# A four-layer mixer on one core: where VectorE does the three operations of a forget-gate group in the softmax half

## The reference, cut to what matters

```python
x = x + linear_attention(layernorm(x))
x = x + ffn(layernorm(x))
x = x + softmax_attention(layernorm(x))
x = x + ffn(layernorm(x))

def ffn(x):                       # the scan runs over the 8 batches, c is 1024 x 256
    def step(c, xt):
        ft = sigmoid(xt @ wf.T + c @ uf.T + bf)
        it = sigmoid(xt @ wi.T + c @ ui.T + bi)
        gt = tanh(xt @ wc.T + c @ uc.T + bc)
        return ft * c + it * gt, None
    c_final, _ = lax.scan(step, c0, x)
    return tanh(einsum('tbi,oi->tbo', x, wo) + c_final @ uo.T + bo)
```

## Time and profile before

| what | us |
|---|---|
| median of three runs | 2560.55 |
| the profiled execution | 2558.81 |
| its span | 2557.0 |
| TensorE busy (matmul) | 2137.9 (84% of the span) |
| VectorE busy | 1692.4 (66%) |
| ScalarE busy | 1266.0 (50%) |
| GpSimd busy | 781.8 (31%) |
| operations of the gates on VectorE in the softmax half | 96 |

### The profile page before, as it was taken

How to read it: one execution, slowest core, us unless ns; L and a number is a source line. 1 busy time by engine, 2 the same in 40 slices (tenths; PEclk the granted TensorE clock), 3 DMA queues, 4 the chain that set the end, 5 groups by cost and what they waited for, 6 DMA issues and landing times.

```text
span 2557.0 us, 58522 instructions
## 1 busy us (share of the span) xinstructions
PE 2137.9 (84%) x24838; PEld 1215.5 (48%) x24838; DVE 1692.4 (66%) x3766; ACT 1266.0 (50%) x2041; POOL 781.8 (31%) x658
## 2 busy tenths in 40 slices
PE   3558989888897985749889999999999999998954
PEld 1346565655565563424345454454544544444432
DVE  5546475656656455348878788787787877777337
ACT  2414343343424221214666666766676666766723
POOL 2132333414133011143424345243352432412110
PEclk9789999899998988877999999999999999999987
DMA  3201010101011011133324133142331322213053
GB/s 97 66 18 43 26 51 18 58 27 51 18 34 35 18 51 50 43 116 99 115 59 126 52 84 117 47 123 66 85 117 35 117 59 76 76 35 97 38 230 131
DMA packets 131540, 179.28 MB, mean 70 GB/s; under 512 B 9120, under 2 KB 95136, under 8 KB 131280
## 3 DMA queue, kind: packets, MB, share of 16 engines
q1 hardware_dynamic: 129104, 175.02, 22.4%
q10 hardware_dynamic: 2176, 0.52, 0.1%
HBM read 97.40 MB, written 77.59 MB: 68 GB/s over the span
## 4 chain that ended last, share of the span: by engine, by line
PE 63%; DVE 24%; ACT 6%; issue 3%; POOL 2%; DMA 1%; SPq 0%; DVEq 0%; POOLq 0%; ACTq 0%
PE general L893 11%; PE general L579 10%; PE out_of_heads L767 9%; DVE maxima L1428 8%; PE scores L722 6%; PE general L565 4%; PE general L904 4%; PE general L545 3%; PE turned_scores L736 3%; PE out_of_heads L653 3%; PE out_of_heads L663 2%; PE scores L611 2%; PE general L553 2%; DVE probs_turned L1375 1%; PE out_of_heads L787 1%
## 5 line engine op out<-in xcount | busy, mean ns | idle before, releaser
L1428 DVE TENSOR_REDUCE maxima<-scores 128x1 f32<-128x512 f32 (+3 forms) x1536 | 793.9, 553 | 239.4 <-PE scores L698 121.3
L1092 ACT ACTIVATE probs_turned<-turned_scores 128x512 f32<-128x512 f32 x1152 | 680.1, 601 | 373.4 <-PE turned_scores L698 190.7
L722 PE MATMUL scores<-k_stacks,q_stacks 59*128 59x512 bf16 (+3 forms) x1536 | 445.3, 336 | 80.9 <-DVE maxima L1428 74.8
L736 PE MATMUL turned_scores<-q_stacks,k_stacks 61*128 61x512 bf16 (+3 forms) x1536 | 437.5, 330 | 2.2 <-ACT probs_turned L1092 2.2
L722 PEld LDWEIGHTS scores<-k_stacks,q_stacks 59*128 59x128 bf16 x1536 | 123.6, 94 | 313.1 <-DVE maxima L1428 247.9
L1749 POOL TENSOR_TENSOR ln_low<-ln 128x512 bf16<-128x512 f32 x128 | 138.4, 1088 | 279.3 <-DVE ln L1410 255.2
L1728 POOL TENSOR_SCALAR ln<-x_for_attention,ln_mean_var,ln_rstd 128x256 f32<-128x256 f32 x104 | 127.9, 1239 | 186.1 <-DVEq L1516 96.9
L1019 ACT ACTIVATE gate_tanhs<-general,feature_vectors 128x512 f32<-128x512 f32 x96 | 66.0, 687 | 204.2 <-PE general L579 199.9
L1664 POOL TENSOR_TENSOR state_low<-state_doubled,state_high 128x2048 bf16<-128x2048 f32 x14 | 57.0, 4068 | 358.1 <-ACT state_high L1025 358.1
L1393 DVE TENSOR_SCALAR reciprocals<-scores 128x16 f32<-128x16 f32 x64 | 11.1, 173 | 224.5 <-PE scores L671 224.5
L767 PE MATMUL out_of_heads<-probs_turned,values 128*17 128x512 f32 (+3 forms) x1536 | 155.2, 499 | 0.0
(11 more groups left out here) (249 smaller groups left out, 5470.8 us busy)
## 6 DMA issues: line engine op xcount, KB each, us to landing
x_after_attention<-x_residual SPq DMA_DIRECT2D x16, 1024.0 KB, 5.2
x_times_wo<-x_wo_out SPq DMA_DIRECT2D x64, 256.0 KB, 2.2
q_stacks<-q_stack SPq DMA_DIRECT2D x64, 256.0 KB, 4.5
k_stacks<-k_stack SPq DMA_DIRECT2D x64, 256.0 KB, 4.8
x_for_attention<-in_x SPq DMA_DIRECT2D x8, 1024.0 KB, 5.5
x_residual<-in_x SPq DMA_DIRECT2D x8, 1024.0 KB, 5.4
x_for_attention<-x_after_attention SPq DMA_DIRECT2D x8, 1024.0 KB, 5.6
ffn_h<-x_times_wo SPq DMA_DIRECT2D x32, 256.0 KB, 6.0
```

Of the source, the lines that this page charges most:

```text
L722: mx = pe.matmul(bank_s[:, first * P:(first + tiles) * P], QS[at_s:at_s + QROWS, r, i * P:(i + 1) * P], KS[at_s:at_s + QROWS, r, k0 * P:(k ...
L736: ex = pe.matmul(bank_t[:, first * P:(first + tiles) * P], KS[at_t:at_t + KROWS, r, j * P:(j + 1) * P], QS[at_t:at_t + KROWS, r, i0 * P:(i ...
L1092: nc.scalar.activation(PR[:, s % SLOTS, :], TB[s % 2][:, :], ACT.Exp).then_inc(sem["ex_taken"], 1)
L1428: r = dve.tensor_reduce(MP[:, gg % 2, g, at:at + 1], max_bank[m][:, first * P:(first + tiles) * P], AX.X, ALU.max)
```

## The change

In the softmax half, `gates(2, ...)` in steps 91, 104, 127 and 140 becomes `gate_op(group, 0)`, `gate_op(group, 1)` and `gate_op(group, 2)` in three consecutive steps: 91 to 93, 104 to 106, 127 to 129 and 140 to 142. The operations, their tiles and their waits are those of before: the wait for three tanh tiles stands ahead of the first, the wait for the second operation stands behind it, and the third raises `gate_used`. The linear half still calls `gates(1, ...)`.

```diff
+            def gate_op(group, n):
+
+                if n == 0:
+                    dve.wait_ge(sem["gate"], w.next("gate", 3))
+                cs = CS[:, group % 2, group // 2 * CH:(group // 2 + 1) * CH]
+                first = gate_place(3 * group)
+                if n == 0:
+                    dve.scalar_tensor_tensor(out=first, in0=first, scalar=1.0, in1=cs, op0=ALU.add, op1=ALU.mult)
+                elif n == 1:
+                    step(dve.scalar_tensor_tensor(out=TG[:, 1, :], in0=TG[:, 1, :], scalar=1.0, in1=TG[:, 2, :],
+                                                  op0=ALU.add, op1=ALU.mult))
+                else:
+                    dve.scalar_tensor_tensor(out=cs, in0=first, scalar=0.5, in1=TG[:, 1, :],
+                                             op0=ALU.mult, op1=ALU.add).then_inc(sem["gate_used"], 1)
...
-                    if k in (91, 104, 127, 140):
-                        gates(2, (91, 104, 127, 140).index(k))
+                    for group, first in enumerate((91, 104, 127, 140)):
+                        if first <= k < first + 3:
+                            gate_op(group, k - first)
```

## The result

The changed kernel takes 2552.29 us (median of seven runs, 2546.39 to 2554.54); the kernel before, 2561.45 us in seven runs beside it. The ratio is 0.9963 (95% interval 0.9954 to 0.9973): 9 to 10 us faster, clear of the noise, and less than half of the 19.9 us forecast. The profiled execution took 2553.2 us, with a span of 2551.4.

A forecast was written before the change was run, and what follows sets the result against it. TensorE held 63% of the chain, standing 27.6 us for maxima behind the gate groups. Gains of 4.1 + 5.8 + 4.5 + 6.2 less 0.7 made 19.9 us, so 2560.55 became 2540.6 us; range 2533 to 2550.

The forecast's parts named there:

- First three groups: Stages 1 to 7: one maximum between operations removes TensorE's waits, gaining 5.8, 4.5 and 4.1 us.
- The end: Stage 8: the third group's last operation stands behind two sums and two additions, losing 0.7 us.
- The fourth group: Stages 1 to 6: step 147 starts at g+7.88 (stage 5, g the first operation's start), not g+8.81; sum 6.2 us gained.
- rival A: Behind the fourth groups, ScalarE's delayed state copy makes TensorE pause, bringing slow clock and no gain there: 2546.9 us, chance 0.12.
- its lower end: Low end of the gain: idle column instead of spacing, fourth group gaining only in stage 4; 10.9 us, 2549.7 us.
- B: Nothing gained: VectorE has the same work and the wait moves to a later maximum; 2560 us, chance 0.05.
- C: Slower: shorter, more frequent TensorE pauses lower its clock behind the first three groups too; 2581 us, chance 0.02.
- D: Fourth group keeps full clock, ScalarE catches up within the stage, all idle time goes: 26.9 us, 2533.7 us, chance 0.07.

The follow-up runs named there:

- the late copy: The whole change plus ScalarE's copy of the state moved from step 143 to step 25 of the next stage, against the kernel before: 2531.28 us, ratio 0.9892.
- the copy in pieces: Kernel before, no group spread, state copy in four 512-column pieces in steps 16, 18, 20 and 24 of the next stage: 2556.63 us, ratio 0.9989.

## Why the prediction was wrong

The forecast was 19.9 us and the stretches of the trace give 8.8. Of the 11 us between them 7.8 are the fourth group's and 3.4 stand behind stage 7.

**First three groups: right.** Forecast 5.8 + 4.5 + 4.1 = 14.4 us, measured 370.0 - 355.5 = 14.5. Each place agrees: 0.87 (forecast 0.88) behind the first group, 0.79 (0.75) behind the second, 0.68 (0.68) behind the third. The two remaining waits of the first group are 0.21 and 0.28 us, the forecast being 0.3 to 0.4.

**The end: right.** Forecast 0.69 us, measured 0.68.

**The fourth group: this term failed.** The forecast said 6.2 us gained; the stretches got 1.6 us longer. Its working was right up to step 145: step 143 at 1.41 us, the copy 3.37 us after the first operation (forecast 3.43) and the exponentials behind it at 5.18 (5.24). The step that failed is the last one: that step 147 follows the exponentials of 145 at g+7.88 whatever TensorE's clock does, so that each stage gains what lies between that and the 8.81 of before. Two things were missing there.

- The transposes in step 146 write a bank that ScalarE's copy of the first transposes (L1085) has to free, and this copy stands in the same queue, behind the state's copy and two exponentials. I counted it in ScalarE's time and not as something that TensorE waits for. That is the 0.45 us, and step 147 at 8.21 us in place of 7.88.
- The clock. The sum set step 147 by ScalarE alone and had no term for a low clock behind the new pauses. In the change the three pauses of 0.68, 1.17 and 0.45 us are followed by low clock in stages 2, 3 and 4 and not in 1 and 5; in stage 6, where no bank is turned, pauses of 0.68, 0.72 and 1.37 us are followed by it too. Over the 11 us from the first operation the clock reads 1.00 in stages 1 and 5 and 0.84 in the four others. The slow part of stage 2 and the same part of stage 5:

```profile
1637.40:1641.80 4.40, 4.00 (x41) 2.27 (x43) 2.33 (x6) 2.83 (x5) 2.60 (x1) 0.61 0.26 51
...
2119.40:2122.80 3.40, 2.99 (x51) 2.01 (x52) 2.28 (x7) 2.75 (x5) 2.62 (x1) 1.00 0.33 65
```

The stretches follow: shorter by 0.6 us in stages 1 and 5 and by 0.5 in stage 4, longer by 0.8, 0.9 and 1.7 in stages 2, 3 and 6. Of the 1.7, about 1.0 us is probably not the fourth group's: stage 6 is that much longer with the first three groups alone too, where a second stretch of low clock stands some 47 us behind the fourth group, as in the change.

Before, the low clock stood behind the single pause of 2.0 us, and TensorE was busy for 3.38 of its 3.40 us, so it cost time there already. The 8.81 that the gain was reckoned from held this cost. Stage 4 of the trace with the first three groups has the fourth in one go at full clock: step 147 at 7.35 us and 106.95 us to the next stage. Stage 1 of the change has it spread at full clock: 8.21 and 107.55. The two stages are alike otherwise (106.46 us each in the trace with the late copy). At the same clock, then, the spreading with the copy in its old place loses 0.6 us, and the 0.6 us that stage 1 gained in the change come from the low clock that is missing there.

This is rival A, to which I gave 0.12, and its time of 2546.9 us is the nearest of the cases. The experiments show its cause: without the copy in the way the same spreading gains (3.6 us lost turn into 12.3 us gained). How much of the loss is the late copy's and how much the clock's differs from stage to stage, and no run holds the clock fixed.

**A term that the sum did not have.** The stretch from stage 7's last group to stage 8's first holds no work that the change moved: the three operations of stage 7's last group have no maxima between them and start 0, 0.61 and 1.33 us into it in both traces. It grew by 3.4 us in the change, and reads 55.3 to 62.9 over the ten traces, with the two traces of the kernel before at 59.6 both. It is not the fourth group's doing alone: with the first three groups spread it already reads 62.2. In the change TensorE's clock is 0.83 and 0.66 in the first two tens of microseconds; before, it is 1.00 in both and low later. Columns as in the earlier trace rows, change and before:

```profile
2420.10:2430.00 9.90, 6.31 (x57) 3.38 (x56) 2.69 (x6) 5.81 (x8) 5.88 (x2) 0.83 0.33 113
2430.00:2440.00 10.00, 7.43 (x49) 5.64 (x50) 2.63 (x4) 1.13 (x2) 0.04 (x1) 0.66 1.01 393
```

```profile
2429.70:2440.00 10.30, 5.59 (x63) 2.87 (x62) 3.36 (x6) 5.97 (x9) 5.92 (x2) 1.00 0.35 124
2440.00:2450.00 10.00, 6.37 (x63) 5.18 (x60) 3.34 (x6) 1.01 (x1) 0.00 (x0) 1.00 1.02 413
```

Over the whole stretch TensorE's busy time grew by as much as the stretch did, before and then change:

```profile
2429.70:2489.30 59.60, 34.10 (x250) 21.48 (x248) 18.23 (x49) 13.12 (x20) 10.38 (x6) 0.83 0.64 247
...
2420.10:2483.00 62.90, 37.46 (x248) 23.86 (x248) 18.20 (x49) 13.16 (x19) 10.38 (x6) 0.78 0.63 234
```

Over the ten traces the clock reads 0.78 in the two longest of these stretches (62.9 and 62.2 us) and 0.88 in the two shortest (55.3 and 56.0). Where the copy was moved, a wait of 1.32 us for exponentials that were queued behind it is gone too. That the lower clock is the 3.4 us is argued from these rows, and no run isolates it. What decides where it falls stays open.

The range was too narrow for the same reason as the forecast: its lower end let the fourth group gain 1.3 us where it could lose, although rival A's mechanism had no floor at zero.

**Rivals B, C, D.** B fell: VectorE's backlog does not come back at a later bank, as the first three groups show. C fell in its place: the first three groups leave no low clock and keep 14.5 us. D did not happen in the change. Its size (26.9 us) is about what the late copy then gave, 26.5 us in its trace, but that is in part chance: 4.3 of these stand behind stage 7, and 8.3 behind the fourth groups of stages 1 to 6, for which D had 12.1.

## What to carry to other kernels

When an engine's operations are spread over steps, the last of them ends later, so look for whoever waits for that last one, and at everything in that engine's queue behind the wait: here one copy, whose result no product used for 68 steps, stood ahead of the exponentials and of the copy that frees a bank. Then follow each of these until the pacing engine is met again, bank by bank, since waits in a row hide each other (3.6 us lost and 2.8 us gained alone, 12.3 us gained together). Where the time of before holds a stretch at the lower clock, ask what the same place takes at full clock, and reckon the gain from both. And where a term rests on an engine just being late enough not to matter, let the range include a loss.

## What was not expected of the hardware

- Low clock behind the fourth group came or did not come with nearly the same timeline. Behind one pause of 2.0 us it came in 22 of 24 places (stages 1 to 6 of the four traces that have it); the exceptions are stage 4 with the first three groups spread and stage 6 with the copy in pieces. Behind the three shorter pauses it came in 8 of 12 (the change and the fourth group alone), in other stages of the one than of the other. Where the copy was out of the way too (four traces), a pause of 0.68 us was left, in stage 6 with one of 0.72 us behind it, and the clock stayed at 1.00 in all 24.
- VectorE's operation with two inputs in SBUF took 1.72 us when it began 0.7 us into GpSimd's operation of 1.89 us, 0.70 us when it began 0.15 us before that operation's end, and 0.68 us with nothing of GpSimd's beside it.
- The same linear half, instruction for instruction, ended within a spread of 5.5 us (1414.7 to 1420.2) over nine traces. A difference of a few microseconds between two traces has to be placed in a stretch before it is explained.
